# A third buffer for key and value weight slices and for the first batch's spread rows, the rows sent by ScalarE's queue, and the weight rounding on VectorE with Sign on ScalarE

## What is computed

```
x = x + tanh(g_xattn[0]) * ssm(ctx, layernorm(x))       # state-space part, 16 states
x = x + tanh(g_ffn[0])   * bit_ffn(layernorm(x))        # rounded weights, 512 -> 2048 -> 512
x = x + tanh(g_xattn[1]) * attention(layernorm(x), ctx) # 16 heads of 128, keys and values from ctx
x = x + tanh(g_ffn[1])   * experts(layernorm(x))        # 4 experts, row r goes to expert r mod 4
```

```
x_dbl = x_proj_w @ u;  Bm, Cm = x_dbl[16:32], x_dbl[32:48]                     # 16 rows each
for t: state = state * exp(d_t * A) + (d_t * u_t) * B_t;  y_t = sum(state * C_t)   # state-space part
gamma_w = clip(mean(abs(w)), 1e-5);  w_dq = clip(round(w / gamma_w), -1, 1) * gamma_w   # three 512 x 2048 matrices
k = ctx @ Wk;  v = ctx @ Wv                                                    # 256 x 2048 each
```

## Time and profile before

| | |
|---|---|
| median of 3 runs | 1866.22 us (1866.08 to 1866.52) |
| profiled execution | 1869.1 us |
| its span | 1867.3 us, 19387 instructions |
| PE busy | 1758.7 us (94%) |
| DVE busy | 1317.8 us (71%) |
| ACT busy | 955.9 us (51%) |
| POOL busy | 663.5 us (36%) |
| DMA | 300.30 MB, mean 161 GB/s |
| chain that ended last | PE 62%, DVE 18%, issue 6%, ACT 5%, DMA 5% of the span |

### The profile page before, as it was taken

One profiled execution on the slowest core, in us unless ns is written; L12 is line 12 of the kernel. 1 busy time (PEld: TensorE's weight loads), 2 busy tenths in 40 slices (PEclk: granted clock), 3 DMA queues, 4 the chain that ended last, 5 costly groups with the idle time before them and its releaser, 6 DMA issues.

```text
span 1867.3 us, 19387 instructions
## 1 busy us (share of the span) xinstructions
PE 1758.7 (94%) x6054; PEld 801.7 (43%) x6054; DVE 1317.8 (71%) x1919; ACT 955.9 (51%) x1904; POOL 663.5 (36%) x693
## 2 busy tenths in 40 slices
PE   8878769989999999999999999999999899999999
PEld 2323233434444344444444544444444344454543
DVE  3978877998998799889887989987643444422221
ACT  6867875656563555575456565564435233330100
POOL 1324522345472244456432464562123333310100
PEclk9989889999999899999999999999999999999999
DMA  8999933688771146697312589841112799846110
GB/s 267 260 289 291 300 109 98 173 211 215 189 195 46 48 102 155 160 266 196 102 31 70 129 199 234 212 109 62 41 47 78 215 301 256 246 141 241 68 51 28
DMA packets 163173, 300.30 MB, mean 161 GB/s; under 512 B 18936, under 2 KB 51704, under 8 KB 160128
## 3 DMA queue, kind: packets, MB, share of 16 engines
q1 hardware_dynamic: 145792, 236.14, 40.3%
q0 software_dynamic: 17280, 62.92, 17.5%
HBM read 177.64 MB, written 58.33 MB: 126 GB/s over the span
## 4 chain that ended last, share of the span: by engine, by line
PE 62%; DVE 18%; issue 6%; ACT 5%; DMA 5%; POOL 2%; SPq 2%; DVEq 0%; ACTq 0%; POOLq 0%
PE p L799 9%; PE p L776 8%; PE p L759 8%; PE p L810 8%; PE p L846 6%; DVE s_M L963 5%; PE p L652 4%; PE p L782 4%; PE p L861 3%; DVE s_M L958 2%; PE p L699 2%; DVE s_M L968 2%; PE p L733 2%; DMA s_bc<-bc_scratch 1%; PE p L738 1%
## 5 line engine op out<-in xcount | busy, mean ns | idle before, releaser
L963 DVE TENSOR_TENSOR_SCAN s_M<-s_M 128x1024 f32<-128x1024 f32 x128 | 296.8, 2319 | 7.8 <-ACT s_M L1218 5.3
L1106 DVE CUSTOM_DVE_ANT_0 s_U<-p,s_U 128x512 f32<-128x512 f32 x256 | 187.3, 745 | 162.8 <-PE p L776 161.5
L776 PE MATMUL p<-s_U 128*128 128x512 f32 x512 | 269.3, 614 | 5.6 <-DVE s_U L1106 2.8
L759 PE MATMUL p<-s_U 128*128 128x512 f32 x512 | 253.7, 604 | 4.7 <-DMA s_U<-in_Wq 2.1
L1445 POOL DMA_DIRECT2D s_u<-s_M x120 | 112.6, 938 | 391.5 <-DVE s_M L968 368.8
L1490 POOL TENSOR_SCALAR s_U<-s_U 128x512 f32<-128x512 f32 x256 | 229.4, 917 | 6.3
L810 PE MATMUL p<-s_U 128*128 128x512 f32 x512 | 224.0, 593 | 0.0
L799 PE MATMUL p<-s_U 128*128 128x512 f32 x472 | 213.6, 593 | 2.6 <-ACT s_U L1348 2.5
L1348 ACT COPY s_U<-p 128x512 f32<-128x512 f32 x196 | 105.3, 592 | 189.7 <-PE p L782 188.4
L1218 ACT ACTIVATE s_M<-s_dl,s_small 128x511 f32<-128x511 f32 x256 | 170.3, 718 | 40.3 <-DVE s_M L963 36.8
L1343 ACT ACTIVATE s_U<-s_U 128x512 f32<-128x512 f32 x256 | 181.6, 710 | 5.3
(11 more groups left out here) (171 smaller groups left out, 2364.3 us busy)
## 6 DMA issues: line engine op xcount, KB each, us to landing
s_u<-s_M POOLq DMA_DIRECT2D x120, 512.0 KB, 7.6
s_bc<-bc_scratch SPq DMA_DIRECT2D x128, 256.0 KB, 5.0
k_scratch<-s_U SPq DMA_DIRECT2D x16, 1024.0 KB, 9.4
v_scratch<-s_U SPq DMA_DIRECT2D x16, 1024.0 KB, 7.8
s_U<-in_Wq SPq DMA_DIRECT2D x64, 256.0 KB, 6.9
s_U<-k_scratch SPq DMA_DIRECT2D x64, 256.0 KB, 5.2
s_U<-rk_scratch SPq DMA_DIRECT2D x64, 256.0 KB, 5.5
s_U<-in_Wo SPq DMA_DIRECT2D x64, 256.0 KB, 4.5
```

Of the source, the lines that this page charges most:

```text
L759: ins = e.matmul(banks[bk][:], wqq[j % 2][:, k, :], axT[b % 2][:, k, :], start=(k == 0), stop=(k == 3))
L776: e.matmul(banks[bk][:], qT[j % 3][:, k * 128:(k + 1) * 128], kT[j % 2], start=True, stop=True).then_inc(S["a_s"], 1)
L963: e.tensor_tensor_scan(w, dA[i % 2], w, 0.0, ALU.mult, ALU.add).then_inc(S["m_s"], 1)
L1106: e.tensor_tensor_reduce(out=Pm[j % 2][:, k, :], in0=banks[ABANK[kind, j, k]][:], in1=rkb[j % 2], scale=rq[:, k:k + 1], scalar=-3.0e38, op ...
```

## The change

It has three parts.

- **Spread rows of batch 0.** They get a third buffer, in the place of fp8 weights that parts 2 and 3 of the third matrix fill, and state n takes buffer n % 3. ACT sends them, not SP: those of states 0 to 2 right behind Softplus, those of n behind the decay of step 2n - 2, after a wait for `m_c` of 2n - 4. Batches 1 to 3 stay with SP and two buffers. The put of part 2 of the third matrix waits for the last product of batch 0, and so does the load of batch 1's context, which waited for the last but one.
- **Rounding.** DVE does multiply and add in one instruction on the part (`rnd`), the clip is gone, and ACT's `put` is Sign of the value minus the constant, with the constant in a column `magic`, written by POOL. Rounding to -1, 0 or 1 is the sign of the rounded value. ACT no longer waits for the threshold.
- **Key and value slices.** Three buffers in turn for key slice 0, value slice 0, key slice 1 and so on. Key slice 1 is loaded at the start; then value slice q + 1 goes where key slice q lay, and key slice q + 2 where value slice q lay.

The steps' costs in the planner follow: `rnd` is DVE 1.25, `clip` has no step, `put` of part 2 needs the last product.

```diff
@@ -61,7 +61,6 @@
...
         QUANT += [("put", w, c - 1)] if c else []
-        QUANT += [("clip", w, c)] if c < 4 else []
     if w == 1:
@@ -311,11 +310,9 @@
...
         elif kind == "rnd":
-            out.append(("Q", [("ACT", 2.0)], [(0, "thr", w, 0)], (0, kind, w, c), [], []))
-        elif kind == "clip":
-            out.append(("Q", [("DVE", 1.3)], [(0, "rnd", w, c)], (0, kind, w, c), [], []))
+            out.append(("Q", [("DVE", 1.25)], [(0, "thr", w, 0)], (0, kind, w, c), [], []))
         elif kind == "put":
-            out.append(("Q", [("ACT", 2.0)], [(0, "clip", w, c)], (0, kind, w, c), [], []))
+            out.append(("Q", [("ACT", 2.0)], [(0, "rnd", w, c)] + ([(0, "out", 2 * NS - 1)] if (w, c) == (2, 2) else []), (0, kind, w, c), [], []))
         else:
@@ -509,6 +507,16 @@
...
 
+        rows = [bcs[i][:] for i in range(2)] + [wq[:, 5 * 4096:6 * 4096].bitcast(F32).rearrange("p (i l) -> p i l", i=2)]
+
+        def spot(b, n):
+
+            return n % 2 if b else n % 3
+
+        def spread_count(b, n):
+
+            return 32 * (n // 3 + 1) if b == 0 else 32 * ((6, 5)[n % 2] + NS // 2 * (b - 1) + n // 2 + 1)
+
         def term(b, i):
@@ -516,7 +524,7 @@
...
         cT = [U[:, 9216 + 1024 * i:10240 + 1024 * i].rearrange("p (t l) -> p t l", t=2) for i in range(NB)]
-        wk, wv = (U[:, o:o + 1024].rearrange("p (k n) -> p k n", k=2) for o in (13312, 14336))
+        wkv = [U[:, o:o + 1024].rearrange("p (k n) -> p k n", k=2) for o in (13312, 14336, 25600)]
         ks = [U[:, 15360 + 2048 * i:17408 + 2048 * i].rearrange("p (h t) -> p h t", h=4) for i in range(NKS)]
@@ -727,15 +735,16 @@
...
                         if b == 0:
-                            e.wait_ge(S["d_kw" if kind == "k" else "d_vw"], 16 * (q + 1))
+                            c = 2 * q + (kind == "v")
+                            e.wait_ge(S[f"d_kv{c % 3}"], 16 * (c // 3 + 1))
                     if kind == "k":
                         for k in range(2):
-                            ins = e.matmul(banks[bk][:], wk[:, k, i * 128:(i + 1) * 128], cT[b][:, k, :], start=(k == 0), stop=(k == 1))
+                            ins = e.matmul(banks[bk][:], wkv[2 * q % 3][:, k, i * 128:(i + 1) * 128], cT[b][:, k, :], start=(k == 0), stop=(k == 1))
                         ins.then_inc(S["k_k"], 1)
...
                         for k in range(2):
-                            ins = e.matmul(banks[bk][:], cT[b][:, k, i * 128:(i + 1) * 128], wv[:, k, :], start=(k == 0), stop=(k == 1))
+                            ins = e.matmul(banks[bk][:], cT[b][:, k, i * 128:(i + 1) * 128], wkv[(2 * q + 1) % 3][:, k, :], start=(k == 0), stop=(k == 1))
                         ins.then_inc(S["k_v"], 1)
@@ -903,9 +912,8 @@
...
                             e.tensor_scalar(r, r, thr[:, w:w + 1], None, ALU.mult).then_inc(S["q_raw"], 1)
-                    elif kind == "clip":
-                        e.wait_ge(S["q_rnd"], 4 * w + c + 1)
-                        e.tensor_scalar(stg[c], stg[c], MAGIC - 1.0, MAGIC + 1.0, ALU.max, ALU.min).then_inc(S["q_cut"], 1)
+                    elif kind == "rnd":
+                        e.tensor_scalar(stg[c], stg[c], thr[:, w:w + 1], MAGIC, ALU.mult, ALU.add).then_inc(S["q_rnd"], 1)
                     elif kind == "bias":
@@ -949,13 +957,13 @@
...
                         if g == 0:
-                            e.wait_ge(S[f"d_bc{n % 2}"], 32 * ((NS * b + n) // 2 + 1))
+                            e.wait_ge(S[f"d_bc{spot(b, n)}"], spread_count(b, n))
                         if i >= NW:
...
                             e.wait_ge(S["m_dl"], 2 * b + g + 1)
-                        e.tensor_tensor(two(wy[term(b, i)[0]]), du[:, 2 * g:2 * g + 2, :], rep(bcs[n % 2][:, 0, :], 2), ALU.mult).then_inc(*v.up())
+                        e.tensor_tensor(two(wy[term(b, i)[0]]), du[:, 2 * g:2 * g + 2, :], rep(rows[spot(b, n)][:, 0, :], 2), ALU.mult).then_inc(*v.up())
                     elif kind == "scan":
@@ -1194,15 +1202,15 @@
...
                         e.activation(junk, stg[c], ACT.Abs, accum_out=wab[:, i:i + 1]).then_inc(S["q_abs"], 1)
-                    elif kind == "thr":
-                        e.wait_ge(S["q_thr"], w + 1)
-                    elif kind == "rnd":
-                        e.activation(stg[c], stg[c], ACT.Copy, bias=MAGIC, scale=thr[:, w:w + 1]).then_inc(S["q_rnd"], 1)
                     elif kind == "put":
...
                         dst = (wqg, wqv)[w][:, c, :] if w < 2 else wqo[:, 4 * c:4 * c + 4, :].rearrange("p t h -> p (t h)")
-                        e.wait_ge(S["q_cut"], i + 1)
-                        e.activation(dst, stg[c], ACT.Copy, bias=-MAGIC, saturate=False).then_inc(S["q_put"], 1)
+                        e.wait_ge(S["q_rnd"], i + 1)
+                        if i == 0:
+                            e.wait_ge(S["p_set"], 9)
+                        if i == 10:
+                            e.wait_ge(S["m_c"], 2 * NS)
+                        e.activation(dst, stg[c], ACT.Sign, bias=magic[:, 0:1], saturate=False).then_inc(S["q_put"], 1)
                     elif kind == "bias" and c < 2:
@@ -1216,6 +1224,12 @@
...
                         e.activation(av[:, t, 1:512], dl[:, 2 * g + t, 1:512], ACT.Exp, scale=Aneg[:, 2 * g + t, n:n + 1]).then_inc(S["m_da"], 1)
+
+                def spread(n):
+                    if n >= 3:
+                        e.wait_ge(S["m_c"], 2 * n - 4)
+                    for i in range(2):
+                        e.dma_start(rows[n % 3][:, i, :], bcd[b, i * NS + n].partition_broadcast(128)).then_inc(S[f"d_bc{n % 3}"], 16)
 
@@ -1241,12 +1255,18 @@
...
                             e.activation(dl[:, 2 * g:2 * g + 2, :], M0[:, 2 * g:2 * g + 2, :], ACT.Softplus).then_inc(S["m_sp"], 1)
+                        if b == 0:
+                            e.wait_ge(S["d_bcw"], 16)
+                            for n in range(3):
+                                spread(n)
                     elif kind == "decay":
...
                         decay(i)
+                        if b == 0 and i % 2 == 0 and 3 <= i // 2 + 1 < NS:
+                            spread(i // 2 + 1)
                     elif kind == "hn":
@@ -1408,6 +1428,7 @@
...
                 e.memset(raw, 0.0).then_inc(S["p_set"], 1)
+                e.memset(magic[:], -MAGIC).then_inc(S["p_set"], 1)
 
@@ -1537,14 +1558,14 @@
...
             def load_kw(q):
+                if q > 1:
+                    e.wait_ge(S["k_v"], 4 * NB * (q - 1))
+                e.dma_start(wkv[2 * q % 3], wd["Wk"][:, :, q * 512:q * 512 + 512]).then_inc(S[f"d_kv{2 * q % 3}"], 16)
+
+            def load_vw(q):
                 if q:
                     e.wait_ge(S["k_k"], 4 * NB * q)
-                e.dma_start(wk, wd["Wk"][:, :, q * 512:q * 512 + 512]).then_inc(S["d_kw"], 16)
-
-            def load_vw(q):
-                if q:
-                    e.wait_ge(S["k_v"], 4 * NB * q)
-                e.dma_start(wv, wd["Wv"][:, :, q * 512:q * 512 + 512]).then_inc(S["d_vw"], 16)
+                e.dma_start(wkv[(2 * q + 1) % 3], wd["Wv"][:, :, q * 512:q * 512 + 512]).then_inc(S[f"d_kv{(2 * q + 1) % 3}"], 16)
 
@@ -1560,6 +1581,7 @@
...
                     e.dma_start(cT[b], ctx_view(b)).then_inc(S["d_cr"], 16)
+                load_kw(1)
                 load_x(0)
@@ -1579,13 +1601,11 @@
...
                 def spread(n):
-                    kk = NS * b + n
-                    if kk >= 2:
-                        e.wait_ge(S["m_c"], 2 * kk - 2)
-                    if n == 0 and b:
+                    e.wait_ge(S["m_c"], 2 * (NS * b + n) - 2)
+                    if n == 0:
                         e.wait_ge(S["m_ip"], 4 * b + 4)
                     for i in range(2):
-                        e.dma_start(bcs[n % 2][:, i, :], bcd[b, i * NS + n].partition_broadcast(128)).then_inc(S[f"d_bc{n % 2}"], 16)
+                        e.dma_start(rows[spot(b, n)][:, i, :], bcd[b, i * NS + n].partition_broadcast(128)).then_inc(S[f"d_bc{spot(b, n)}"], 16)
 
@@ -1595,12 +1615,13 @@
...
                     elif kind == "sp":
-                        e.wait_ge(S["d_bcw"], 16 * (b + 1))
-                        spread(0)
-                    elif kind == "mul" and i % 2 == 0 and i < 2 * NS - 2:
+                        if b:
+                            e.wait_ge(S["d_bcw"], 16 * (b + 1))
+                            spread(0)
+                    elif b and kind == "mul" and i % 2 == 0 and i < 2 * NS - 2:
                         spread(i // 2 + 1)
                     elif kind == "add" and i == 2 * NS - 2 and b + 1 < NB:
-                        e.wait_ge(S["m_c"], 32 * b + 2 * NS - 1)
+                        e.wait_ge(S["m_c"], 32 * b + (2 * NS - 1 if b else 2 * NS))
                         e.dma_start(bcs[0][:], ctx_view(b + 1)).then_inc(S["d_cb"], 16)
@@ -1622,13 +1643,13 @@
...
                         if b == NB - 1 and q < 3:
-                            load_kw(q + 1)
+                            load_vw(q + 1)
```

(22 more changed lines are left out.)

## The result

| | median | ratio to before, 95% interval |
|---|---|---|
| before | 1866.37 us (1866.08 to 1866.99) | |
| after | 1878.07 us (1875.52 to 1879.4) | 1.0058 [1.0042, 1.0074] |

The change costs 0.6%, where I forecast a gain of 0.9%. The profiled execution of after took 1875.5 us, its span 1873.7. It is the fastest of the four, and the profiled one of before (1869.1) is slower than its timed ones, so the two traces hold 6.4 of the 11.7 us between the medians.

The account below looks back on a forecast made before the run. DMA was taken to bound the first stage, PE from 260 us. Transposes: 257.8 - 17 + 4 - 7 = 238 us; PE gains 15 + 2 = 17, so 1852.1 profiled, 1849 median; forecast case 1842 to 1858, range 1832 to 1868.

Parts of the forecast that it names:

- The planner's new order: Every engine's order, worked out anew from changed costs and needs: taken as 0, with 5 us to either side.
- Spread waits, 17 us: DVE's waits for batch 0's spread rows: 17 of 20.9 us won back, between 8 and 20.
- Rival 2: DVE's wait moves to the accumulating DMA in batch 0; 15 of 20 us return, 1862 us; chance 0.21.
- Late start, 4 us: Batch 0's first spread rows, sent by ACT only behind Softplus: 4 us lost, between 1 and 7.
- ACT's issues, 16 us on ACT: ACT's 32 spread sends in batch 0: 16 us of ACT time, bounds 10 and 47.
- rival 3: ACT's issues block decays and PE's bank copies, 47 us on ACT; slower, 1880 us; chance 0.12.
- rival 4: Sign isn't in Exp's table, so ACT's puts take table loads, 31 us; ends near 1870; chance 0.05.
- The 7 us: Rounding without the DVE-ACT ping-pong at batch 0's thresholds: 7 us gained, bounds 0 and 8.
- Slices: Third key/value slice buffer: PE's 10.6 + 3.2 us of waits go, with 2.05 + 2.8 us of slowed matmuls.
- PE's gain: PE, the bound from 260 us, gains 20 - 10 + 5 (clock) = 15 us from batch 0's earlier transposes.
- at most 5 of the 6: PE's 6.0 us wait at 407 us for DVE's batch 0 rows: at most 5 go; 2 counted.
- The stores: Key and value stores issued by batch 0's transposes: 19 to 21, 21 before; 10 us of PE work moves behind.

Follow-up runs that it names:

- e5: Kernel before, every instruction unchanged, with one need added in the planner so that every engine's written order changes; 1878.29 us, 1.0094.
- e8: All three parts of the change in the kernel before's written order, third spread buffer in space free until attention; 1862.79 us, 0.9991 of before.
- e10: The changed kernel with POOL, not SP, sending the key scales; 1868.88 us, 1.001 of before.
- e16: e8 with e5's added need in the planner and POOL sending the key scales; 1859.58 us, 0.9976 of before.
- e6: Kernel before in its written order, plus only the ACT-sent third spread buffer, in space free until attention; 1863.92 us, 1.0004.
- e7: Kernel before in its written order, plus only the rounding on DVE with Sign on ACT; 1862.66 us, 0.9985.
- e3: Kernel before plus only the third buffer for key and value slices; 1862.44 us, 0.9985.
- e4: The changed kernel with batch 0's spread rows sent by SP again, three buffers kept; 1872.82 us, 1.0022 of before.

## Why the prediction was wrong

- **The planner's new order: the step that failed.** I wrote "no row shows what that does, and I give it 0, with 5 us to either side". A new order alone costs 0.94% [0.6, 1.29], some 13 to 17 us (e5), as much as the whole gain that I had summed, and between e8 and the changed kernel lie 12 us. With the orders come 29.7 us of SP's halts before 262 us in after (0.7 in e8), and one of 13.1 us at the end of the keys in e5. My list of what stands behind each moved wait stopped at the instructions that the diff names. The store of the key scales isn't among them, and the rows of before show it harmless (1.2 us before 262 us), so it looked safe. The edit that takes the halt away brings the change back to 1.001 (e10). Nor does "after 430 us PE lost only 24 of 970 us" bound it: in e5 PE waits 7.8 us for Wq right at that edge.
- **Spread waits, 17 us: right as a wait, wrong as a gain.** 20.9 fell to 1.2. In e8, without the new order, 18.9 of 19.5 us came back under other names. The wait that decided batch 0's end was that for the third matrix's Abs, 3.4 us, and in e8, with the spreads on time, it grew to 9.1. I had a reason for this in my first paragraph, 102% of the DMA engines, and used it for the keys only, not for DVE's chain: with the spreads asked for earlier, the third matrix landed later. Rival 2 had this with one name (accumulations, 15 us back, 1862). e8, at 0.9991 of before, is within its 1858 to 1868; its name came true in e16 (15.1 us), while in e8 the Abs had most of it.
- **Late start, 4 us: nothing.** ACT's sends went out from 35.90 us on, two of the three pairs ahead of Softplus at 37.64. The first product is at 42.34 and the first scan at 45.77, for 42.16 and 45.87.
- **ACT's issues, 16 us on ACT (rival 3, 47 us): none on ACT's compute that the trace shows.** They take 0.45 us in the median, 1.55 at most, and run beside ACT's own instructions (below). In e6 DVE's waits for ACT did grow, for decays from 2.3 to 11.5 us and for roundings from 2.0 to 7.6. ACT waits 11.6 us there for stores of keys to land; whether the issues have a share isn't shown.
- **Rounding.** DVE's multiply-add took 1.28 us for 1.22, Sign 2.01, and no table load stood by a Sign: rival 4 falls, and with it the reading of the Trainium skill (ScalarE: Activation LUTs, section "Table sets: the hidden batching unit") under which it was possible. The 7 us were nearly right for batch 0's end: it comes 5.8 us earlier in e7, this part in the old order. But e7 is only 0.15% faster, 2 to 3 us.
- **Slices: right as a wait, wrong as a gain.** 10.6 + 3.2 us of PE waits went (in e3 and e8; in after one of 7.9 remained, behind SP's halt). But in e3 PE's waits for ACT, which frees the PSUM banks, grew from 18.4 to 31.8 us before 262 us, the largest group of them

```profile
PE p L745 <- ACT s_U L1319: 12.9, 6, 7.7
```

  so PE was busy only 1.9 us more from 50 to 260, the granted clock stayed at 0.90 (I had counted 5 us for it), and e3 is 0.15% faster at best.
- **PE's gain, "PE is the bound from 260 us": right in the old order, wrong in the new.** In the nine kernels with the order of before, the entry follows the transposes by 149.2 to 151.4 us, so what comes earlier at 258 us comes out earlier at 407. The wait of 6.0 us for DVE stays, 6.0 to 6.7 us in all nine, so the "at most 5 of the 6" weren't to be had. In the changed kernel's order, PE's 12.6 us of extra work before 260 bought idle time (123.1 of 140 us busy) and no time.
- **The stores**: 24 key and value stores issued by 262 us for 22 before, not fewer; batch 0 also ends 11.7 us later, so this says little on the 10 us that I took off.
- **A sum within the chances**: of rival 2's 1858 to 1868 less than half lies below 1862.5, taken evenly, not two thirds; "faster" was then 0.71, not 0.76.

The sum I should have made, from the runs: order +0.9% or more, all content together -0.1%. The changed kernel's own order is yet another one, with its own halts, so the +0.6% isn't exactly that sum.

## What to carry over

When every engine runs a written order and a planner makes it, test the new order by itself, with the old instructions, before any content is judged: here it cost 0.9% alone. For a stage that several engines share, find the step after which the rest takes a fixed time; a wait ahead of it is worth only what that step gains. Look for the instruction in a shared DMA queue whose wait is for another engine's late, unimportant result; let the engine that makes the result send it. And where the DMA engines are as full as here (0.92 from 50 to 260 us), count bytes: 20.9 us of waits for spread rows moved to other names when the rows were asked for earlier, and 4 MB less ended batch 0 8.7 and 10.5 us sooner.

## What the runs showed of the hardware

- DMA issues from ACT's queue run beside ACT's instructions, and can run ahead of ones that stand before them in the program. From ACT's order of time in after (s_wq is the third spread buffer's place):

```profile
35.90 0.81 ACTq L1232 DMA_DIRECT2D s_bc<-bc_scratch  x2
36.35 1.28 ACT L1257 ACT_TABLE_LOAD   x1
36.74 0.94 ACTq L1232 DMA_DIRECT2D s_bc<-bc_scratch  x2
37.64 1.06 ACT L1257 ACTIVATE s_dl<-s_M 128x1024 f32<-128x1024 f32 x1
37.71 1.82 ACTq L1232 DMA_DIRECT2D s_wq<-bc_scratch  x2
```

  The sends are written behind both Softplus instructions, and two pairs start before the first. They wait for no semaphore that Softplus signals. Over 0 to 262 us:

```profile
L1232 ACTq DMA_DIRECT2D s_bc<-bc_scratch x22: 326/449/1552, 35.9 to 232.0; - x22
```

- A third queue that sends cost nothing by itself in the old order (e6, 1.0004 [0.9989, 1.002]). In the changed kernel's order it goes with 0.36 points (e4, 1.0022 for 1.0058), whose place no trace shows.
- A saturated set of DMA engines moves 294 GB/s over 170 us, in before, in e8 (49.9 MB) and in e16 (50.1 MB) alike, whichever queues send. In the changed kernel, with SP's halts, it is 272.
